# Two PSUM banks exchanged, line products moved one place, the residual added on VectorE, and fewer zero fills

## The reference, cut to what matters

```
h = layernorm(x) * (1 + ca) + sa
q, k, v = h @ w_qkv.T + b_qkv
w = exterior(h_prev @ w1_write.T, h @ w2_write.T)      # 6 numbers a head, normalised
r = exterior(h @ w1_read.T, h @ w2_read.T)
bias = (r . J w) * decay ** (q - k) * [q > k] * bias_scale
attn = softmax(q k / sqrt(8) + bias, causal)
x = x + ga * ((attn @ v) @ w_out.T + b_out)            # the residual of this change
h2 = layernorm(x) * (1 + cb) + sb
x = x + gb * sum over the top 2 experts of p_e * (silu(h2 W1) * (h2 W2)) W3
```

## Time and profile before

| | |
|---|---|
| median of three runs | 1112.42 us (1110.73 to 1112.75) |
| profiled execution, its own time | 1111.9 us |
| its span, first to last instruction | 1110.2 us |
| PE, DVE, ACT, POOL busy, share of the span | 84%, 70%, 65%, 73% |
| setup ends | about 31.9 us |
| first and last exponential of attention | 96.8 and about 822 us |
| experts begin | about 863 us |

### The profile page before, as it was taken

How to read it: one execution, slowest core, us unless ns; L and a number is a source line. 1 busy time by engine, 2 the same in 40 slices (tenths; PEclk the granted TensorE clock), 3 DMA queues, 4 the chain that set the end, 5 groups by cost and what they waited for, 6 DMA issues and landing times. The chain is left out here.

```text
span 1110.2 us, 30824 instructions
## 1 busy us (share of the span) xinstructions
PE 935.1 (84%) x9473; PEld 742.2 (67%) x9473; DVE 775.5 (70%) x2067; ACT 721.6 (65%) x1612; POOL 811.7 (73%) x1352
## 2 busy tenths in 40 slices
PE   2346899889999899998999989998872799999967
PEld 2335677767777777777777777776652688888852
DVE  8576668777777777777777777777746466555536
ACT  2435678887778877888787887876562455555520
POOL 8366668888888888888888888887435366666644
PEclk9997999999999999999999999998985899999989
DMA  7336556565666656666566665655411353333339
GB/s 189 114 110 161 150 139 172 152 178 137 168 159 158 172 147 160 161 158 173 143 163 159 153 178 146 163 156 157 118 44 49 79 168 93 91 91 91 83 138 357
DMA packets 233854, 160.39 MB, mean 144 GB/s; under 512 B 57376, under 2 KB 220512, under 8 KB 233568
## 3 DMA queue, kind: packets, MB, share of 16 engines
q1 hardware_dynamic: 222416, 133.77, 46.0%
q0 software_dynamic: 8448, 17.45, 5.1%
q10 hardware_dynamic: 2832, 7.20, 1.7%
HBM read 81.38 MB, written 76.19 MB: 142 GB/s over the span
## 5 line engine op out<-in xcount | busy, mean ns | idle before, releaser
L919 DVE TENSOR_REDUCE peak<-pre 128x6 f32<-128x768 f32 x256 | 244.5, 955 | 116.4 <-PE pre L759 113.5
L1151 ACT ACTIVATE PT<-sc 128x768 f32<-128x768 f32 x256 | 204.6, 799 | 35.3 <-PE sc L746 32.9
L950 DVE TENSOR_TENSOR sc<-sc,decay 128x512 f32<-128x512 f32 x256 | 177.5, 693 | 30.4 <-PE sc L730 25.3
L1637 POOL DMA_INDIRECT yab<-y_out,xt x136 | 131.4, 966 | 82.8 <-issue 63.4
L1359 POOL DMA_INDIRECT xg<-stage,slot_i x128 | 130.9, 1022 | 62.9 <-issue 26.8
L759 PE MATMUL pre<-causal,identb 128*128 128x256 bf16 x512 | 144.7, 283 | 0.0
L758 PE MATMUL pre<-KT,queries 84*128 84x256 bf16 x512 | 143.5, 280 | 0.0
L757 PE MATMUL pre<-KT,queries 84*128 84x128 bf16 x512 | 116.5, 228 | 20.4 <-DMA queries<-line_rows 12.6
L1591 DVE TENSOR_TENSOR hid<-silu,up 128x256 f32<-128x256 f32 x136 | 57.3, 421 | 82.0 <-ACT silu L1545 82.0
L743 PE MATMUL sc<-queries,KT 99*128 99x128 bf16 x512 | 101.6, 223 | 13.2 <-issue 6.8
L1545 ACT ACTIVATE silu<-up 128x256 f32<-128x256 f32 x136 | 52.2, 384 | 88.4 <-PE up L1481 88.4
(11 more groups left out here) (279 smaller groups left out, 2731.9 us busy)
## 6 DMA issues: line engine op xcount, KB each, us to landing
line_rows<-line_part SPq DMA_DIRECT2D x64, 216.0 KB
dim_rows<-dim_part SPq DMA_DIRECT2D x64, 192.0 KB, 2.1
KT<-dim_rows SPq DMA_DIRECT2D x64, 192.0 KB
queries<-dim_rows SPq DMA_DIRECT2D x64, 192.0 KB
line_rows<-line_part SPq DMA_DIRECT2D x64, 144.0 KB
KI<-line_rows SPq DMA_DIRECT2D x64, 144.0 KB
QI<-line_rows SPq DMA_DIRECT2D x64, 144.0 KB
xt<-xg SPq DMA_DIRECT2D x136, 65.0 KB, 1.9
```

What stands on the lines that cost most here:

```text
L919: nc.vector.reduce_max(peak[half][:, i:i + 2, 0:3], pre[:, :, 0:3 * P].rearrange("p n (g k) -> p n g k", g=3), AX.X)\
L950: nc.vector.tensor_tensor(seeded(p), seeded(p), decay[:, 2 * p:2 * p + 2, :].unsqueeze(2).broadcast_to([P, 2, NT, P]), ALU.mult).then_inc( ...
L1151: nc.scalar.activation(PT[p % 4][:], sc[:, window], ACT.Exp).then_inc(exped.sem, 1)
L1637: nc.gpsimd.indirect_dma_start(yab, bass.IndirectOffsetOnAxis(xt[r][:, D:D + 1].bitcast(i32), 0), y_out[r % 8][:], None).then_inc(y_sent[r ...
```

## The change

- `JOBS`: `lines` goes from position 0 to position 1 of place 1, so behind `prescores`. `out` goes to bank 1, `norm2` to bank 0 (they exchange).
- `res` is now two transposes of `yT` into PSUM; the two products with x are gone. ScalarE's copy (L1124) is gone too; VectorE adds the bank to `x_all` in place, just ahead of the statistics.
- The maxima's rows go from 96 to 84, right behind the lines. So the rows between are no longer read, and only the token halves that no line row fills are zeroed: in `setup` VectorE's six fills become two of half the size, and on GpSimd two of the four fills become half the size.
- In `setup`, GpSimd makes `key_mask` earlier, and VectorE copies it into `KI` before the turned weights instead of at its end.

```diff
-PEAK0 = 96
+PEAK0 = DIMS + LINES
 JOBS = [
-    (1, 0, "lines", 3, 0), (1, 1, "head1", -1, 1),
+    (1, 1, "lines", 3, 0), (1, 1, "head1", -1, 1),
...
-    (4, 1, "out", -1, 0), (4, 1, "norm2", -2, 1),
+    (4, 1, "out", -1, 1), (4, 1, "norm2", -2, 0),
...
+        def pairs(tile):
+            return tile[:].rearrange("p h t -> p (h t)").bitcast(u32).rearrange("p (h t) -> p h t", h=H)
...  (GpSimd, setup; the three lines on key_mask move up to here from behind identb)
+                nc.gpsimd.memset(query_mask[0][:], MASK)
+                step(nc.gpsimd.memset(key_mask[0][:], 1.0))
+                nc.gpsimd.affine_select(out=key_mask[1][:], ...).then_inc(key_mask_ok, 1)
...
                 for m in range(2):
-                    step(nc.gpsimd.memset(v["KT"][m][64:96].rearrange("p h t -> p (h t)").bitcast(u32), 0))
-                    step(nc.gpsimd.memset(v["KT"][m][96:P].rearrange("p h t -> p (h t)").bitcast(u32), ones_pair))
+                    step(nc.gpsimd.memset(v["KT"][m][64:96].rearrange("p h t -> p (h t)").bitcast(u32), ones_pair))
+                    step(nc.gpsimd.memset(pairs(v["KT"][m])[0:PEAK0, :, P // 2:P], 0))
...  (VectorE, setup)
                 for m in range(2):
-                    nc.vector.memset(v["KT"][m][32:64].rearrange("p h t -> p (h t)").bitcast(u32), 0)
-                    nc.vector.memset(v["QF"][m][32:64].rearrange("p h t -> p (h t)").bitcast(u32), 0)
-                    nc.vector.memset(v["QF"][m][64:96].rearrange("p h t -> p (h t)").bitcast(u32), 0)
+                    nc.vector.memset(pairs(v["QF"][m])[0:PEAK0, :, 0:P // 2], 0)
...  (the copy into KI, moved up to behind the first use of logit)
+                dve.wait_ge(key_mask_ok, 1)
+                nc.vector.tensor_copy(v["KI"][0:MR]..., key_mask[1][:]...)
                 dve.wait_ge(wT_ok, 1)
...  (TensorE, job "res")
                         wait(pe, used["out"], jb)
-                        settle(pe, pe_settled)
                         for t in range(NT):
                             blk = slice(t * P, (t + 1) * P)
-                            nc.tensor.matmul(B[:, blk], ident[:], x_all[:, span(jb * T + t * P, P)], start=True, stop=False)
-                            last = nc.tensor.matmul(B[:, blk], yT[:, blk], ident[:], start=False, stop=True)
+                            last = nc.tensor.transpose(B[:, blk], yT[:, blk], ident[:])
...  (VectorE, extras at place 7)
                         jb = b - 1
+                        wait(dve, ready["res"], jb)
+                        rows = x_all[:, span(jb * T, T)]
+                        nc.vector.tensor_tensor(rows, rows, bank[BANK["res"]][:, 0:T], ALU.add).then_inc(used["res"].sem, 1)
                         wait(dve, used["res"], jb)
...  (ScalarE)
-                    elif name == "res":
-                        nc.scalar.activation(x_all[:, span(jb * T, T)], B[:, 0:T], ACT.Copy).then_inc(done, 1)
```

More of the change, by code:

```diff
@@ L273, in _ @@
                                         pattern=[[-1, P]], channel_multiplier=1).then_inc(ident_ok, 1)
+                nc.gpsimd.memset(query_mask[0][:], MASK)
+                step(nc.gpsimd.memset(key_mask[0][:], 1.0))
+                nc.gpsimd.affine_select(out=key_mask[1][:], in_=key_mask[0][:], compare_op=ALU.is_ge, fill=0.0, base=-1,
+                                        pattern=[[1, P]], channel_multiplier=-2).then_inc(key_mask_ok, 1)
                 step(nc.gpsimd.iota(dist_i[:], pattern=[[1, P]], base=0, channel_multiplier=-1))
@@ L305, in _ @@
                 ones_pair = 0x3F803F80
[L306 to L309, removed]
                 step(nc.gpsimd.affine_select(out=query_mask[1][:], in_=query_mask[0][:], compare_op=ALU.is_ge, fill=0.0, base=0,
@@ L392, in _ @@
                 nc.vector.tensor_tensor(az[:], logit[:], lam2[:], ALU.max).then_inc(az_ok, 1)
+                dve.wait_ge(key_mask_ok, 1)
+                nc.vector.tensor_copy(v["KI"][0:MR].rearrange("p h (t k) -> p (h t) k", t=NT),
+                                      key_mask[1][:].unsqueeze(1).broadcast_to([MR, H * NT, P]))
                 dve.wait_ge(wT_ok, 1)
@@ L435, in _ @@
                 last.then_inc(arg_ok, 1)
-                dve.wait_ge(key_mask_ok, 1)
-                nc.vector.tensor_copy(v["KI"][0:MR].rearrange("p h (t k) -> p (h t) k", t=NT),
-                                      key_mask[1][:].unsqueeze(1).broadcast_to([MR, H * NT, P]))
                 dve.wait_ge(out_bias_ok, 1)
@@ L514, in attend @@
         used = {j: signal("used_" + j) for _, _, j, _, _ in JOBS}
-        sp_settled, dve_settled, pool_settled, act_settled, pe_settled, init = (
-            sem(n) for n in ("sp_settled", "dve_settled", "pool_settled", "act_settled", "pe_settled", "init"))
+        sp_settled, dve_settled, pool_settled, act_settled, init = (
+            sem(n) for n in ("sp_settled", "dve_settled", "pool_settled", "act_settled", "init"))
         stats, var, rstd, shift, normed = signal("stats", 2), signal("var"), signal("rstd"), signal("shift"), signal("normed")
@@ L1172, in body @@
                         for name, jb in [job for place in range(3) for job in jobs_at(b, p, place)]:
-                            if name[:-1] != "head" and name not in ("route", "rank", "norm2") and (name != "v" or b < 0):
+                            if name[:-1] != "head" and name not in ("route", "rank", "norm2", "res") and (name != "v" or b < 0):
                                 evacuate(name, jb, jb % 2)
```

## The result

Twenty runs of each kernel: 1114.31 us median after (1110.04 to 1126.18), 1110.84 before (1102.47 to 1116.02). The ratio is 1.0053, with a 95% interval of 1.0032 to 1.0074: the change makes the kernel slower by half a per cent, some 6 us (the medians alone differ by 3.5). The forecast was 1105.3 us, with a range of 1099.5 to 1111.

A forecast was written before the change was run, and what follows sets the result against it. The prediction took GpSimd's own chain to bound the kernel. From the profiled 1111.9 us, setup -3.0, first batches -1.2, steady part -1.0 and end -1.4 sum to -6.6, so 1105.3 us, range 1099.5 to 1111.

The forecast's parts named there:

- What bounds the kernel: Steady attention batches: GpSimd's own chain sets the 22.7 us batch, not TensorE, though TensorE is busier.
- Line products, 0 us in a steady batch: Place 1 of attention: later line products cost 0 us per steady batch, up to +1.11 us each in first batches.
- the rival in which it makes the clock fall: TensorE's standstill at place 1 drops the clock in most batches: +14.3 us, about 1120.6 us in all; chance 0.06.
- Steady part, -1.0: Steady attention: TensorE's added spare time shortens GpSimd's eight true waits, 2.2 us in all, by 1.0 us.
- the price of a fall, 0.55 us: Steady attention: each fall of TensorE's granted clock was read as costing 0.55 us of GpSimd waits.
- Rows 84 instead of 96, 0 us: Attention's scores: moving the maxima's rows leaves as many matmuls and columns, so 0 us.
- Setup, -3.0: Before attention: smaller fills and the moved `KI` copy end setup 3.0 us earlier; bounds -5.4 and -0.2.
- Banks, 0: Steady batch: `head0` no longer waits for `h2T`, but most is waited for again later: 0 us; bounds -0.55 and 0.
- Residual: `res` in a steady batch: TensorE saves 0.57 us, VectorE adds 0.42, covered by GpSimd's chain: 0 us.
- -1.4 was put: End of attention, last sequence: `res` to statistics shrinks from 2.64 to about 1.2 us, a gain of 1.4 us.
- -1.2 was put for residual and line products together: First batches, before GpSimd binds: `res` savings less later line products give -1.2 us; bounds -2.5 and +1.5.

## Why the prediction was wrong, point by point

- **What bounds the kernel** was right. Undisturbed batches are 22.9 us with every edit that leaves GpSimd's work alone, and one outer product less took 17.4 us of 18 expected. The 22.7 us of the prediction come from counting 22 batches in 500 us; GpSimd's instruction comes every 22.9 us before, too.
- **Line products, 0 us in a steady batch:** this is the step that failed. It cost 13.8 us in this company. The wait of over a microsecond was foreseen, and so was the rival in which it makes the clock fall, which was given 0.06. The rival's mechanism is the one that the runs show, but that its term of +14.3 us is near to the 13.8 is luck: it reckoned with a fall in each of 26 batches at 0.55 us, and the profile has seven, four of which cost 6.1 us. The reason against it, that 1.21 us before `head0` seldom lets the clock fall, does not carry over: the wait for the rows is as long as a DMA is late, up to 2.35 us, and a fall makes the next batch's loads late. That the wait can be so long was in the earlier trace rows, where it was 2.11 us.
- **Steady part, -1.0, and the price of a fall, 0.55 us:** the price was about right where a fall stands alone, 0.65 us before; four batches in a row cost 6.1 us after. TensorE's spare time did not make falls cheaper in the changed kernel.
- **Rows 84 instead of 96, 0 us:** wrong. It counted matmuls and columns. By the runs it is 5.7 us in the changed kernel, measured against 128 partitions, and about 10 in the setup part alone, where the fills differ too.
- **Setup, -3.0:** -2.1. The port's other direction decided: the copy stopped GpSimd for 2.0 us.
- **Banks, 0:** 4 us gained alone. "Most of it is waited for again one step later" held for the batch, but the shorter standstill is worth something by itself; the profile without a fall points to the clock.
- **Residual:** 0 in undisturbed batches held. From `res` to the statistics 1.3 us were gained where -1.4 was put, but the whole end gained some 4, and the first batches 1.0 to 2.2 where -1.2 was put for residual and line products together. The whole, 7.9 us alone, was undersized.
- **Sum:** with the line products back and 128 partitions the changed kernel measures 0.9911, a gain of 9.9 us, more than the 6.6 forecast. The place of the line products turns it into 1.0002 (10.1 us), the 87 partitions that into 1.0053 (5.7 us). The parts don't add: alone they sum to 0.0006, together they are 0.0053. So the two terms that were put at 0 us, the line products and the rows, turned a gain into a loss.

## What to carry to other kernels

An engine that has time to spare is not free to stand still: before you move TensorE's work from ahead of a wait to behind it, ask how long it then stands, whether the wait is for a DMA that a late batch makes later, and what it runs next at half the clock. Work that fills such a gap can be worth more than work saved. When the time of a kernel varies from run to run, price a step by many runs and read the profile for the mechanism alone.

## What the runs showed of the hardware

The kernel before, with products of the same columns and the same duration (0.22 us) over 128 partitions instead of 99, the added ones zero in `QF`, measured 0.9959 of its time (0.9937 to 0.9981), in a kernel where TensorE stands still 1.2 us in each batch; its profile had no fall of the granted clock between 200 and 740 us, where the profile over 99 had four. In the setup part alone, 87, 99 and 128 partitions gave 1.0057, 0.9963 and 0.9957, with other fills in the first. In the changed kernel falls of the granted clock to 0.50 came with standstills of 1.7 to 2.4 us in four batches in a row. VectorE's cast of 64x4096 from SBUF to SBUF held up a GpSimd cast of 128x128 that began 0.1 us after it: 2.33 us instead of 0.29.
